# Shared feed-forward of an MoE block: four chunks early and seven late, with a one-chunk middle team

## What is computed

```python
w = weights[subjects]                                   # one 64x64 map for each of 64 batches
xf = einsum('bct,bcd->bdt', x, w).reshape(4096, 512)    # the "front": tokens of 512 values
combine = top 2 of softmax(xf @ gate_w.T) over 8 experts
y = sum over the two chosen experts of combine * (silu(xf @ fc1_e.T) * (xf @ fc2_e.T)) @ proj_e.T   # 352 wide
shared = silu(xf @ shared_fc1.T) * (xf @ shared_fc2.T) @ shared_proj.T                              # 1408 wide
out = x + y + sigmoid(xf @ shared_gate_w.T) * shared
```

## Time and profile before

| | us |
|---|---|
| median of three executions | 1248.91 (1248.50 to 1249.07) |
| profiled execution, its own time | 1247.88 |
| its span, first to last instruction | 1246.1 |
| TensorE busy | 1234.0 (99%) |
| VectorE busy | 819.2 (66%) |
| ScalarE busy | 463.8 (37%) |
| GpSimd busy | 264.8 (21%) |

### The profile page before, as it was taken

The page is one execution under the profiler, slowest core; times in us unless marked ns, Lnnn a source line. Parts: engine busy times, 40 slices in busy tenths (PEclk is TensorE's granted clock), DMA queues, the critical chain, the costliest instruction groups (busy, mean ns, idle before and its releaser), DMA issues.

```text
span 1246.1 us, 17282 instructions
## 1 busy us (share of the span) xinstructions
PE 1234.0 (99%) x6208; PEld 1025.6 (82%) x6208; DVE 819.2 (66%) x1331; ACT 463.8 (37%) x765; POOL 264.8 (21%) x356
## 2 busy tenths in 40 slices
PE   9999999999999999999999999999999999999998
PEld 7888888888888899988888888888787887787887
DVE  6444554469754777776666665557678778678675
ACT  5223231221011566665555554446314213213211
POOL 4277774000001111111111111110232130130110
PEclk9999999999999999999999999999999999999999
DMA  9488876212205677686666566743895875875842
GB/s 338 156 287 286 315 277 253 88 39 102 102 35 209 231 239 263 226 280 210 203 207 214 201 214 203 253 138 128 287 320 169 314 252 177 268 261 166 293 136 102
DMA packets 105411, 262.94 MB, mean 211 GB/s; under 512 B 11090, under 2 KB 11218, under 8 KB 100850
## 3 DMA queue, kind: packets, MB, share of 16 engines
q1 hardware_dynamic: 67602, 164.74, 37.5%
q0 software_dynamic: 13872, 54.27, 13.2%
q10 hardware_dynamic: 23856, 42.87, 10.4%
HBM read 195.52 MB, written 66.32 MB: 210 GB/s over the span
## 4 chain that ended last, share of the span: by engine, by line
PE 90%; DVE 6%; issue 1%; ACT 1%; DMA 1%; ACTq 0%; DVEq 0%
PE bank_h L938 41%; PE bank_o L938 24%; PE bank_h L1197 9%; PE bank_t L1197 6%; PE bank_t L915 2%; PE bank_h L1079 2%; PE bank_t L938 2%; PE bank_t L862 1%; PE bank_o L872 1%; DMA x_hi<-late_up 1%; PE bank_h L872 0%; PE bank_h L883 0%; DVE rawp L1941 0%; DVE h_lo L1719 0%; DVE h_sb L1715 0%
## 5 line engine op out<-in xcount | busy, mean ns | idle before, releaser
L938 PE MATMUL bank_h<-x_hi,w_hi 128*128 128x512 f32 (+1 forms) x768 | 278.6, 363 | 0.0
L938 PE MATMUL bank_h<-x_hi,w_lo 128*128 128x512 f32 (+1 forms) x768 | 272.2, 354 | 0.0
L938 PE MATMUL bank_h<-x_lo,w_hi 128*128 128x512 f32 (+1 forms) x768 | 272.0, 354 | 0.0
L820 POOL DMA_INDIRECT rows<-xf_rows,token_of x71 | 69.2, 975 | 551.7 <-PE bank_t L915 370.4
L938 PE MATMUL bank_o<-wp_hi,h_hi 128*128 128x512 f32 (+1 forms) x442 | 180.8, 409 | 1.2 <-DVE h_lo L1719 1.2
L938 PE MATMUL bank_o<-wp_lo,h_hi 128*128 128x512 f32 (+1 forms) x442 | 178.0, 403 | 0.0
L938 PE MATMUL bank_o<-wp_hi,h_lo 128*128 128x512 f32 (+1 forms) x442 | 177.8, 402 | 0.0
L938 PEld LDWEIGHTS bank_h<-x_hi,w_lo 128*128 128x128 f32 x768 | 145.2, 189 | 20.7
L938 PEld LDWEIGHTS bank_h<-x_hi,w_hi 128*128 128x128 f32 x768 | 145.5, 189 | 18.3 <-DVE x_lo L1723 0.7
L938 PEld LDWEIGHTS bank_h<-x_lo,w_hi 128*128 128x128 f32 x768 | 145.5, 189 | 17.6
L1838 DVE TENSOR_TENSOR w_lo<-raw,w_hi 128x640 fp32r<-128x640 f32 (+1 forms) x116 | 93.5, 835 | 39.9 <-ACT w_hi L1259 39.9
(11 more groups left out here) (269 smaller groups left out, 2326.1 us busy)
## 6 DMA issues: line engine op xcount, KB each, us to landing
raw<-ew SPq DMA_DIRECT2D x29, 1408.0 KB
w_early<-late_up ACTq DMA_DIRECT2D x69, 256.0 KB
slot_rows<-res SPq DMA_DIRECT2D x32, 512.0 KB, 3.4
rawp<-ewp SPq DMA_DIRECT2D x29, 512.0 KB
x_hi<-late_up ACTq DMA_DIRECT2D x46, 256.0 KB, 3.9
x_lo<-late_up ACTq DMA_DIRECT2D x46, 256.0 KB
xt_in<-xf_transposed SPq DMA_DIRECT2D x11, 1024.0 KB, 7.3
late_up<-raw POOLq DMA_DIRECT2D x6, 1792.0 KB, 8.2
```

The lines of the kernel that those rows point to most:

```text
L820: pool.indirect_dma_start(rows[:, row % 4, :], None, xf_dram, bass.IndirectOffsetOnAxis(token_of[:, HALF_OF[row]:HALF_OF[row] + 1].bitcast ...
L938: mm = pe.matmul(dst, a, m, start=(first and i == 0), stop=(last and i == 2))
```

## The change

One chunk goes from the early part to the late part: four early, seven late. Seven late chunks are three teams: three chunks, one chunk (`MIDDLE` = 3), three chunks. The middle chunk has its eight rows not behind its products but one each behind later products of the next two chunks, and VectorE adds them there. Its down weights take the place of chunk 0's and are loaded in every block, and chunk 0's after them again.

The front's slots no longer end with chunks: the block's 48 product steps (`STEPS` = 32 in stage 1, 16 in the rows) are counted, and `MAPS_AT` gives the step behind which each of the eight maps stands. Transposes and router products go two at a time, the transposes behind the second and third step of a slot, the router products behind its last two. The rows 0 and 1 are made together, their last chunk last. GpSimd's preparation begins at tile `PREP` = 8 with four tiles a chunk, and chunk 6 follows behind the loop. In the expert part a few transposes stand some matmuls later, and in the last expert tile and the late picks the order of ScalarE and VectorE differs.

```diff
-PARTS = [list(range(0, 5)), list(range(5, 11))]
+PARTS = [list(range(0, 4)), list(range(4, 11))]
+MAPS_AT = ((4, 9, 14, 19, 25, 31, 39, 47), (7, 12, 17, 21, 26, 31, 39, 47))
+STEPS = 2 * KC * len(PARTS[0])
-TEAMS = LATE // TEAM
+TEAMS = 3
+MIDDLE = TEAM
-PREP = TILES - 3 * LATE
+PREP = TILES - 4 * (LATE - 1)
...
GpSimd, loop over tiles
-                j, part = divmod(t - PREP - 1, 3)
+                j, part = divmod(t - PREP - 1, 4)
                 if j >= 0:
                     pool.wait_ge(late.summed, 4 * j + 4)
-                    at_least(pool, late.split_lo, 4 * j + (0, 3, 4)[part])
+                    at_least(pool, late.split_lo, 4 * j + (0, 1, 3, 4)[part])
...
                 elif t >= PREP and part == 1:
                     late_split_sums(j)
+                elif t >= PREP and part == 2:
                     late_split_raw(j)
                 elif t >= PREP:
                     late_split_down(j)
+            late_sums(LATE - 1)
+            late_split_sums(LATE - 1)
+            late_split_raw(LATE - 1)
+            late_split_down(LATE - 1)
...
TensorE
+            def front_step(b, step, slots):
+                first = isinstance(b, int) and b == 0
+                maps = MAPS_AT[first]
+                k = next(q for q in range(SLOTS) if step <= maps[q])
+                begin, end = maps[k - 1] + 1 if k else 0, maps[k]
+                t = LEAD + SLOTS * b + k
+                at = step - begin
+                if k <= slots and at in (1, 2):
+                    for c in (2 * at - 2, 2 * at - 1):
+                        front_transpose(t - 1, k - 1, c, bank_t[1])
+                if k <= slots + 1 and step >= end - 1:
...
+                        front_route(t - 2, k - 2, c, bank, xt_in[:, t - 2, c * P:(c + 1) * P] if first and k < 2 else None)
+                if k < slots and step == end:
+                    front_slot_map(b, k)
...
-            def shared_row(n, b, r, front=0):
+            def shared_rows(n, b, after_row=None, front=0):
...
+                order = [(r, j) for r in range(2) for j in range(chunks - 1)] + [(r, chunks - 1) for r in range(2)] + [
+                    (r, j) for r in range(2, BT) for j in range(chunks)]
+                for step, (r, j) in enumerate(order):
+                    if j == 0:
+                        at_least(pe, f.o_kept, b * BT + r - 1)
...
-            shared_step(0, FULL + 2, at({4: table(0)}), at({1: table(1)}))
-            shared_step(0, FULL + 3, at({0: table(2), 2: table(3), 3: table(4), 4: table(5)}), at({0: table(6)}))
+            shared_step(0, FULL + 2, at({3: table(0)}), at({2: table(1)}))
+            shared_step(0, FULL + 3, at({0: table(2), 1: table(3), 2: table(4), 3: table(5)}), at({1: table(6)}))
+            shared_step(0, BLOCKS - 1, at({0: table(7)}), at({1: [first_turns]}))
...
-                    if k == 0:
+                    if k == (1 if turned_late(i) else 0):
                         single_transpose(i)
...
+                late_rows(b, 0)
+                late_chunk(b * LATE + MIDDLE)
+                late_chunk(b * LATE + MIDDLE + 1, ((), (), (0,), (1,), (2,), (3,), (4,)))
+                late_chunk(b * LATE + MIDDLE + 2, ((5,), (6,), (7,), (), (), (), ()))
+                late_chunk(b * LATE + MIDDLE + 3)
...
ScalarE, gates and shared_step
+                    if front:
+                        for k in (((0,), (1, 2), (3,), (4,)), ((), (1,), (2, 3), (4,)))[first][j]:
+                            if k < front:
+                                front_slot(b, k)
                     act.wait_ge(f.h_full, b * chunks + j + 1)
...
-                for k in range(len(PARTS[0]), late):
+                late = 7 if isinstance(b, int) and b == 0 else 6
+                for k in range(5, min(late, front)):
                     front_slot(b, k)
                 split_xt(n, b + 1)
...
VectorE, front and late
+            def front_block(b, slots):
...
+                    slot_fx(b, k, slots)
+                    if first and k in (0, 3):
+                        split_shared(0, 3 if k else 2)
+                    if k == 6:
+                        one_hidden(0, b, 3)
...
+                    if k == 6:
+                        dve.wait_ge(gate_ready, b + 1)
+                        dve.wait_ge(res_loaded, 16 * (b + 1))
+                        for r in range(2):
+                            row_sum(0, b, r)
...
             late_x_lo(0, P1)
+            expert_hidden(XT - 1, 0)
             late_x_lo(0, P6)
+            expert_hidden(XT - 1, 1)
             late_sum(0, 3)
-            for j, p in enumerate((P7, P5, P2)):
-                expert_hidden(XT - 1, j)
+            expert_hidden(XT - 1, 2)
+            for p in (P7, P5, P2, P4, P3):
                 late_x_lo(0, p)
...
-                    if r % 2 == 0:
-                        ahead = 2 if b else 0
-                        at_least(dve, late.o_kept, b * TEAMS * HROWS + min(r, ahead + r // 2) + 1)
-                        late_pick(HROWS * b + ahead + r // 2)
-                for j in range(TEAM):
-                    if b == 0:
-                        late_pick(BT + j)
-                    elif j != 1:
-                        late_pick(HROWS * b + 6 + j // 2)
+                    if r in ((0, 2, 4, 6) if b else (0, 2, 3, 4, 5, 6)):
+                        late_pick(HROWS * b + (2 + r // 2 if b else max(r - 1, 0)))
+                for j in range(MIDDLE, LATE):
+                    if j in (MIDDLE, LATE - 1):
+                        late_pick(HROWS * b + (6 if j == MIDDLE else 7))
                     if b + 1 < HBLOCKS:
-                        for q in ((0,), (1, 2), (3,))[j]:
-                            late_sum(b + 1, q)
-                    late_chunk(b * LATE + TEAM + j)
+                        late_sum(b + 1, j - MIDDLE)
+                    late_chunk(b * LATE + j)
```

More of the change, by code:

```diff
@@ L680, in _ @@
                     n = b * LATE + j
+                    if j == MIDDLE:
+                        sp.wait_ge(late.o_full, (TEAMS * b + 1) * HROWS)
+                        load_late_wp(1, MIDDLE, 1)
+                    if j == LATE - 1 and b + 1 < HBLOCKS:
+                        sp.wait_ge(late.o_full, (TEAMS * b + 2) * HROWS)
+                        load_late_wp(0, 0, 1)
                     if j == 0:
@@ L1229, in late_part, with middle_rows @@
                 c = slice(r * P, (r + 1) * P)
-                m = product(late_bank[row % 3][:, :], (late_h[0][:, jj, c], late_h[1][:, jj, c]),
-                            (late_wp(0, j), late_wp(1, j)), jj == 0, jj == TEAM - 1)
-                if jj == TEAM - 1:
+                at = late_slot(j)
+                m = product(late_bank[row % 3][:, :], (late_h[0][:, at, c], late_h[1][:, at, c]),
+                            (late_wp(0, j), late_wp(1, j)), jj == 0, jj == last)
+                if jj == last:
                     m.then_inc(late.o_full, 1)
+            def middle_rows(b, rows):
+                for r in rows:
+                    if r == 0:
+                        pe.wait_ge(late.wp_in[1], 32 * (b + 1))
+                    late_part(b, 1, r, 0)
             def late_rows(b, g):
@@ L1737, in rest_xt, with one_hidden, hiddens @@
                                         ).then_inc(shared[n].x_lo, 1)
-            def hiddens(n, b, ahead=0, between=None, front=0):
+            def one_hidden(n, b, j):
                 f, chunks = shared[n], len(PARTS[n])
-                for j in range(chunks):
-                    if ahead and j + ahead < chunks:
-                        split_shared(n, j + ahead)
-                    if front:
-                        front_slot(b, j, front)
-                    g = slice(j % 2 * BN, (j % 2 + 1) * BN)
-                    hidden(f, b * chunks + j, (h_hi[:, j, :], h_lo[:, j, :]), h_sb[:, g], bank_h[2 * (j % 2) + 1][:, :], g_sb[:, g])
+                g = slice(j % 2 * BN, (j % 2 + 1) * BN)
+                hidden(f, b * chunks + j, (h_hi[:, j, :], h_lo[:, j, :]), h_sb[:, g], bank_h[2 * (j % 2) + 1][:, :], g_sb[:, g])
+            def hiddens(n, b, between=None):
+                for j in range(len(PARTS[n])):
+                    one_hidden(n, b, j)
                     if between:
                         between(j)
+            def front_block(b, slots):
+                first = isinstance(b, int) and b == 0
+                for k in range(SLOTS):
+                    slot_fx(b, k, slots)
[3 more added lines that the diff above has]
+                        one_hidden(0, b, 3)
+                    elif first and k in (1, 4):
+                        one_hidden(0, b, k // 2)
+                    slot_xt(b, k, slots)
+                    if first and k == 2:
+                        one_hidden(0, b, 1)
+                    elif not first and k in (1, 3, 4):
+                        one_hidden(0, b, k // 2 if k < 4 else 2)
+                    if k == 6:
[3 more added lines that the diff above has]
+                            row_sum(0, b, r)
+                    if k == 7:
```

(15 more changed lines are left out.)

203 lines of the change are left out of this document (104 added, 99 removed).

## The result

The changed kernel takes **1253.54 us** in the median of six runs (1251.93 to 1256.02), the kernel before 1248.18 us (1246.71 to 1249.07): a ratio of 1.0043, with a 95% interval of 1.0033 to 1.0054. It is slower by over 0.2%, in the range, and not the case that was held likeliest. The profiled execution of the changed kernel took 1251.93 us with a span of 1250.1, that of before 1247.88 and 1246.1: 4.0 us more span.

A forecast was written before the change was run, and what follows sets the result against it. TensorE, busy 99% of the span, was taken as the bound, with GpSimd nearly as late in the front. Saved matmuls (-5.4) and added waits summed to +2.3 us: 1251.2 against the median, stated as 1251.0, range 1245 to 1257.

The forecast's parts named there:

- the case that was held likeliest: Whole kernel: time within 0.2% of the kernel before, forecast 1251.0 us; chance 0.38.
- front, net of block 2's wait: Blocks 0 to 3: +4.5 us of TensorE waiting for GpSimd's map copies, less the 0.6 us wait of before.
- row 2's wait in blocks 3, 4, 5: Row 2 needs row 0's bank back one product after row 0 is full: 0.27 us in each block, +0.8.
- row 3 of block 4: Row 3 needs row 1's sum, which VectorE makes after `rest_xt` and `route_weights`: +2.1 us.
- table 0: Block 5: table now behind four chunks, at 21.8 us, but VectorE's chain ends 24.4 us after the start: +2.6 us.
- experts and late part: Expert tiles and late part: waits of 0.93 and half of 1.60 go, moved transposes give 0.3, rows add 0.6: -1.4 us.
- TensorE waits 188.9 - 184.4 = +4.5 us in the front: Last front map, tile 31: GpSimd's copies ready at 188.9, TensorE wants them at 184.4; range 0 to 12 us.
- I cost it at nothing while GpSimd holds TensorE, and at up to 2 us if it doesn't: Front: ScalarE's table load and sigmoid now ahead of the copy of slot 5's rows, 1.28 us and more.
- The rule on the shared interfaces: Front: VectorE instructions with two SBUF inputs contend with GpSimd; 0.5 us more a cycle would make the sum 1254.
- GpSimd keeps up: Front costs 2 us at most in place of 4.5: 1246.5 and down to 1245 us; chance 0.26.
- GpSimd by far: Front: GpSimd's cycle is 26.2 us and sums start at 46, 12 us behind TensorE: 1258.5 us; chance 0.26.
- The late part is VectorE's: Late part: `late_row` makes sums of results late, 1 to 1.5 us four times: 1255 to 1257 us; chance 0.10.

The follow-up runs named there:

- the second run: The changed kernel with `route_weights` of block 4 behind row 1's sum in place of row 0's: 1250.63 us, ratio 1.0024 to the kernel before.
- the first run: The changed kernel with table 0 of block 5 moved from behind the fourth chunk to behind row 1: 1251.49 us, ratio 1.0021 to the kernel before.

## Why the prediction was right or wrong

In us, on the profiled executions; idle times with the 0.16 on top:

| term | forecast | shown | by |
|---|---|---|---|
| 24 matmuls | -5.4 | -5.4 | count 6184 |
| front, net of block 2's wait | +3.9 | +4.2 | seven idle times, 4.9, for 0.7 before; wrong releaser |
| spacing of matmuls up to the last map | 0 | +1.3 | 41.5 us for 40.2; cause open |
| the same behind that map | 0 | about -1.4 | low clock apart; cause open |
| row 2's wait in blocks 3, 4, 5 | +0.8 | +1.3 | 0.44, 0.44, 0.41 |
| row 3 of block 4 | +2.1 | +2.0 | wait at 245.97, taken away in the second run |
| table 0 | +2.6 | +2.7 | wait at 274.91, taken away in the first run |
| the 0.25 at 311.98 | -0.3 | -0.4 | gone |
| experts and late part | -1.4 | about -1.9 | sums of the waits |
| low clock | none | +1.7 | stretch at 247 |
| sum | +2.3 | +4.1 | span +4.0 |

- **The sum's closeness** is in part luck: its +2.3 was to be GpSimd's 4.5 us and is other engines' 4.2, and two terms that it did not have, +1.3 and -1.4 of spacing, cancel.
- **The matmuls, row 3, table 0**: right in mechanism, place and size. What the sum had not was that the two waits are one chain: taken away one at a time they bring back 0.7 to 1.5 us at the next place, and together 2.3.
- **"TensorE waits 188.9 - 184.4 = +4.5 us in the front", for `blk_ready`**: this step failed. GpSimd's own times were right to 1 us, and the front did lose 4.9 us. But 184.4 was taken with no other wait in the front, and the waits that came were VectorE's: its order and the new place of the last map (`x_lo`, 1.9 us), and ScalarE's order together with subtractions that GpSimd's held up (`h_lo`, 1.9 in three places, 0.7 for rows and 0.3 at a map). "I cost it at nothing while GpSimd holds TensorE, and at up to 2 us if it doesn't" was the wrong way round: the other waits came first, and their cost hid GpSimd's. With those orders mended GpSimd holds TensorE 2.1 us; with its earlier start as well the time is 5.3 us lower, some 3.5 once 1.7 us is taken off each run for each low stretch that its clock shows (an estimate); its earlier start alone is worth nothing that can be told. The largest piece, 1.75 us for `x_lo` of block 1, was not in the sum at all: with the last map at the block's last step, the subtraction that stood behind the last logits had no cover left.
- **The rule on the shared interfaces** (the Trainium skill, GPSIMD Engine Reference, Specifications): the cycle was 25.4 us and not 0.5 over the forecast, so the sum by that rule, 1254, is near the result for another reason. But "the trace bears it out little" looked at GpSimd's cycle alone, and VectorE is the one that pays. Of its 48 subtractions `w_lo` and `h_lo` of 128x512 in the front, the 32 with none of GpSimd's two-input instructions beside them take 0.68 to 0.78 us, in the kernel before as in the changed one; of the 16 with one, 14 before and 12 in the changed kernel take over 0.85, up to 2.77. Before, one wait came of them: the 0.56 us at 173.01 of the earlier trace rows, behind a `w_lo` of 1.77 us at 171.10. This agrees with the rule; no run takes GpSimd's instructions away to show it.
- **Row 2's wait**: right in mechanism, undersized by 0.5 in three, because each wait costs TensorE 0.16 us more than its figure in brackets.
- **Experts and late part**: the 0.93 and the 1.60 of the earlier trace rows are gone, all of the latter where half was taken. What gave some back is ScalarE's results between the experts, six waits of 0.2 us (1.2) that were under 0.15 each before.
- **The low clock** is the term that was missing. It takes the case from the border of "within 0.2%" to plainly slower. The profiled execution has one such stretch. Of the six runs three have a mean clock of 0.999 (1251.9 to 1253.4), two 0.997 (1253.6 and 1254.6), one 0.996 (1256.0): one stretch is 3.4 / 1250 at half the clock, 0.0014, so these are one, two and three of them. Taking 1.7 us off each run for each stretch leaves 1250.2 to 1251.7, 1250.8 on the mean (an estimate from these runs), 0.2% over the kernel before, where the sum said 1250.2 on the profiled execution and 1251.2 against the median.
- **The rivals**: "GpSimd keeps up" was right that it was ahead, by 1.6 us, and wrong that the front would then cost 2 us at most. "GpSimd by far" did not come; it takes 1.1 us more a chunk to show GpSimd in the waits. "The late part is VectorE's" fell: its waits for the sums there are 1.0 us, where before they were 2.5.

## What to carry to other kernels

When a stage gets fewer matmuls, list for each engine what stands in its queue ahead of the thing that TensorE wants next, and price the order and not only the amount of work: here one subtraction in the wrong place cost 1.9 us, about as much as the engine with the fullest queue costs once that is mended. Ask also of each engine whose work moves what it runs beside: GpSimd kept its own times and made VectorE's longer. Chains of waits on one engine are one term: take away its first wait and look at where it comes back. And a wait of 2 us is not 2 us: count the low clock that may come behind it, which also makes a kernel's runs lie further apart.

## What the runs showed of the hardware

**The clock.** An idle time of TensorE of about 2 us can be followed by 3.4 us in which the granted clock is 0.50, 1.2 GHz in place of 2.4, though matmuls stand in a row there: 1.7 us on top. It came behind 1.8 us in block 4 of the changed kernel and behind two of four equal pauses put into the kernel before, whose own runs nearly all keep a clock of 1.000. Once, at 1.5 us, it lasted 7 us. Not each such idle time has it. Between their starts and ends the twelve profiled executions have 25 idle times of 1.5 to 3.2 us (as in brackets). Nine have a low stretch that begins in them or up to 1.2 us behind, the longest has none, and no low stretch lies elsewhere: none at the shorter idle times, of up to 1.3 us. The same wait can go either way: that for `x_lo`, 1.75 us, has none in the changed kernel and one where GpSimd starts earlier; the one before the table has none in the changed kernel and one where the front's order is mended. What decides between them is not settled.

**VectorE beside GpSimd.** A VectorE subtraction of 128x512 with both inputs in SBUF that meets one of GpSimd's two-input instructions can stand until that one ends: 1.65 us in place of 0.69 beside 1.34 us of GpSimd's, 2.8 beside its 2.7 (128x1024). In these cases VectorE's ends 0.55 us behind GpSimd's (157.73 and 158.28 in the changed kernel). Beside GpSimd's casts, with one input, it takes 0.68 to 0.78 us.
